# A two-layer transformer: the gated network's last product moved from VectorE to POOL, with a PSUM copy on ScalarE

## The chip, the core and the metric

One core of a Trainium2 chip runs the kernel: TensorE (PE, with its weight loads shown as PEld), VectorE (DVE), ScalarE (ACT), GpSimd (POOL) and SyncE (SP), which here only issues DMAs. The metric is the device time of one execution in microseconds, the median of several runs. POOL reads and writes SBUF only in this kernel; PE writes the eight PSUM banks of 128x512 f32, and DVE and ACT read them.

## What is computed

The input is 8 sequences of 256 tokens with 128 features. Two layers follow each other, and each is attention and then a feed-forward network, both with a residual sum. The last network is the gated one that the change touches:

```python
# layer 0: x = x + attention0(layernorm(x));  x = x + relu(layernorm(x) @ W1 + b1) @ W2 + b2
# layer 1: x = x + attention1(layernorm(x)), 16 heads of 8, not causal
def _L1_ffn_ref(x, w_gate, w_up, w_down):      # HIDDEN = 384
    wg = _dequant(w_gate, x.dtype)             # integers times 1/127
    wu = _dequant(w_up, x.dtype)
    wd = _dequant(w_down, x.dtype)
    gate = jnp.einsum('bsd,hd->bsh', x, wg)
    up = jnp.einsum('bsd,hd->bsh', x, wu)
    h = jax.nn.silu(gate) * up
    return jnp.einsum('bsh,dh->bsd', h, wd)
# x = x + _L1_ffn_ref(layernorm(x), ...)
```

## The kernel before

The kernel is written engine by engine; each engine's program is a fixed order of instructions, and semaphores hold the engines to each other. Nothing is scheduled by a planner.

The work runs in phases `i = -1 .. 18`. Phases 0 to 7 carry the attention of layer 0 for sequences 0 to 7, phases 8 to 15 that of layer 1. Each phase has 16 slots `s`, one for each head. In a slot, PE writes the scores of the next phase's head s (`scores`, lines 812 to 816, three banks in turn) and the transposed, shifted scores of this phase's head s (`shifted`, lines 834 to 838, two banks in turn). DVE takes the maxima of the first (`maximum`, L654 in layer 1), ACT the exponential of the second (`exp`, L497, output `PB`). Since there are two banks for the shifted scores, `shifted(i, s)` waits until the exponential of slot s-2 is done; since there are three for the scores, `scores(i+1, s)` waits for the maximum of slot s-3. After slots 6, 10 and 14, and in slot 1 of the next phase, PE multiplies four heads' probabilities by V (`pv`, L860).

The rest of a sequence's work is laid between the slots of the phases that follow its attention. For layer 1 it is this:

- one phase later (its attention being phase i-1): slot 3, PE turns the outputs (`turn_o`, L869) and DVE divides them (`norm_o`, L661 and L663, output `Y`); slot 4, POOL adds `Y` to the stream `xs` (L415); slot 5, DVE's statistics; slot 6, POOL's normalisation (`norm`, L351 to L361); slot 10, PE transposes (L765), ACT and DVE make the two f16 parts `XHL`;
- two phases later: in slots 3, 6 and 12 PE computes part j = 0, 1, 2 of the gated network (`ffn1_in`, L927: the gate half in columns 0 to 255 of a bank, the up half in columns 256 to 511) and ACT takes the tanh of the gate half (L554, output `TH`); in slots 4, 7 and 13 DVE does the part's two operations (`hidden`): `GA = (TH + 1) * gate` (L675) and `HG = GA * up` (L678), the second of which empties the bank;
- three phases later: slot 0, PE's last product (`ffn1_out`, L935), and DVE adds it to the stream (`add_stream`, L670). The store of the sequence waits for that sum.

So sequence c has its gated parts in phase c+10 and its last product in phase c+11. Phases 10 to 14 have all the work of a slot, phase 15 has no scores of a next phase any more, and phases 16, 17 and 18 have no attention at all: only the rest of sequences 5, 6 and 7. Parts 0, 1 and 2 use banks 7, 6 and 7; the turned outputs (`oT1`) and the transposed norm (`xT3`) use bank 6 too.

`GA` has two buffers, taken by `j % 2`. The silu is made of a tanh, since silu(g) = g (1 + tanh(g/2)) / 2; the constants are in the weights of the last product.

Of the kernel before, what the change touches and what calls it, by code (L numbers as in the profile page):

```python
# [7 lines left out]
ALU = mybir.AluOpType  # L8
# [8 lines left out]
P = 128  # L17
B, S, D = 8, 256, 128
# [73 lines left out]
def program(nc, x, w0, tab, small, w1, wint, ident, masks, out):  # L92
    with ExitStack() as ctx:
        def sb(name, shape, dt=F32):
            return ctx.enter_context(nc.sbuf_tensor(name, shape, dt))

        def sem(name):
            return ctx.enter_context(nc.semaphore(name))
# [55 lines left out]
        HR = sb("HR", [P, NI, S])  # L154
        TH = [sb(f"TH{j}", [P, S]) for j in range(NG)]
        GA = [sb(f"GA{j}", [P, S]) for j in range(2)]
        HG = sb("HG", [P, NG, S])


# [40 lines left out]
        s_res = sem("x_plus_attention_1")  # L200
        s_hr = sem("ffn0_hidden")
        s_xhi = sem("normedT_3_hi")
        s_th, s_ga = sem("gate_tanh"), sem("gate_silu")

        block = ctx.enter_context(nc.Block())

# [131 lines left out]
        def _(pool):  # L338
# [17 lines left out]
            def norm(n, b):  # L356
                p = b % 2
                rstd(n, b)
                pool.wait_ge(s_rstd[n], 3 * b + 3)
                for t in range(TPB):  # L360
                    ins = pool.tensor_scalar(XN[n][p][:, t], xs[:, b * TPB + t], NMN[:, n, p, t:t + 1],  # L361
                                             RS[:, n, p, t:t + 1], ALU.add, ALU.mult)
                ins.then_inc(s_xn[n], 1)
# [8 lines left out]
            def spread_v(i):  # L372
# [7 lines left out]
                                           va_(b).rearrange("q t (c f d) -> q t c f d", f=2, d=HD)[:, :, :, e])  # L380
                ins.then_inc(s_vp, 1)

            def cut(i, s):

                pool.wait_ge(s_e, H * i + s + 1)

                pool.tensor_tensor(HELD[:, s:s + 1], EPSC[:, 0, 0:1], EPSC[:, 0, 0:1], ALU.add)  # L387
                r = s % RING
                pr = PB[:, r - 1:r + 1].rearrange("q u (n k) -> q (u n) k", n=2)[:, :, 0:P]
                pool.affine_select(out=pr, in_=pr, compare_op=ALU.is_ge, fill=0.0, base=0, pattern=[[0, 4], [1, P]],  # L390
                                   channel_multiplier=-1).then_inc(s_cut, 1)
# [15 lines left out]
            for i in range(-1, NPH + 3):  # L407
                L0, L1, L2 = [phase(i - n)[0] for n in range(3)]
                b1, b2 = [phase(i - n)[1] for n in (1, 2)]
                for s in range(H):  # L410
# [7 lines left out]
                        pool.tensor_tensor(halves(ZG), halves(Y), row(gate_row), ALU.mult).then_inc(s_zg, 1)  # L418
                    if s == 6 and L1 == 1:
                        norm(3, b1)  # L420
                    if s == 7 and i + 1 < NPH:
                        spread_v(i + 1)
                    if s == 8 and L2 == 0:
# [20 lines left out]
        def _(act):  # L444
# [62 lines left out]
            for i in range(-1, NPH + 3):  # L507
                L1, L2 = [phase(i - n)[0] for n in (1, 2)]
                b1, b2 = [phase(i - n)[1] for n in (1, 2)]
                for s in range(H):  # L510
# [40 lines left out]
                    if s in (3, 6, 12) and L2 == 1:  # L551
                        j = (3, 6, 12).index(s)
                        act.wait_ge(*filled(f"gu{j}", b2))
                        act.activation(TH[j][:, :], psum(f"gu{j}", b2)[:, 0:S], ACT.Tanh, scale=0.5 * SCALE).then_inc(s_th, 1)  # L554
                    for b, a in STAGE_A.items():
                        if a["xT"] == H * i + s:
# [19 lines left out]
        def _(dve):  # L576
# [95 lines left out]
            def hidden(c, j):  # L672
                m = psum(f"gu{j}", c)
                dve.wait_ge(s_th, NG * c + j + 1)
                dve.scalar_tensor_tensor(out=GA[j % 2][:, :], in0=TH[j][:, :], scalar=1.0, in1=m[:, 0:S],  # L675
                                         op0=ALU.add, op1=ALU.mult).then_inc(s_ga, 1)
                dve.wait_ge(s_ga, NG * c + j + 1)
                dve.tensor_tensor(HG[:, j], GA[j % 2][:, :], m[:, S:2 * S], ALU.mult).then_inc(*empties(f"gu{j}", c))  # L678

            for i in range(-1, NPH + 3):  # L680
                L1, L2, L3 = [phase(i - n)[0] for n in (1, 2, 3)]
# [64 lines left out]
        def _(pe):  # L746
# [181 lines left out]
                ins.then_inc(*fills(f"gu{j}", c))  # L928

            def ffn1_out(c):  # L930
                pe.wait_ge(*emptied("gu2", c))
                m = into("dn", c)
                for t in range(TPB):
                    for n in range(NG):
                        ins = pe.matmul(m[:, t * D:(t + 1) * D], HG[:, n, t * P:(t + 1) * P], WD[:, n],  # L935
                                        start=(n == 0), stop=(n == NG - 1))
                ins.then_inc(*fills("dn", c))
# [112 lines left out]
```

## Time and profile before

| | us |
|---|---|
| median of 3 runs | 359.61 (358.93 to 360.91) |
| the profiled execution | 359.73 |
| its span in the trace | 358.0 |
| PE busy | 299.5 (84%) |
| DVE busy | 258.4 (72%) |
| ACT busy | 220.4 (62%) |
| POOL busy | 156.4 (44%) |

The span runs from the first instruction to the last; the 1.73 us between it and the execution's time lie around it. An engine's busy time is the union of its instructions. Matmuls are pipelined, and their ends are modelled: a row of a matmul that lasts 0.27 us may be followed by the next one 0.11 us later. So starts are read, not ends, where PE's pace is asked for. Rows of a timeline begin with the start and the duration in us; consecutive instructions of one line may be merged into one row (x2, x3), whose duration is that of the group. In brackets stands the engine's idle time before the row and what released it.

### The profile page before, as it was taken

What the parts mean: (1) busy time and instruction counts of PE and PEld (TensorE: products, weight loads), DVE (VectorE), ACT (ScalarE), POOL (GpSimd) and SP (SyncE); (2) the same over time, 40 slices, a digit from 0 to 9 for tenths busy, and PEclk for the clock granted to TensorE, in tenths of its full rate; (3) what the DMA queues carried; (4) which work ended last, traced back from release to release, by engine and by line L of the source; (5) the groups of instructions that cost most, each with busy time, mean ns of one, the idle gap of its engine ahead of it and who ended that gap; (6) DMA issues with size and microseconds to landing.
All of it is one profiled execution on the core that took longest, in us unless ns stands there. A gap on an engine that the chain in (4) does not pass through costs nothing.

```text
span 358.0 us, 8359 instructions
## 1 busy us (share of the span) xinstructions
PE 299.5 (84%) x2832; PEld 210.3 (59%) x2832; DVE 258.4 (72%) x1009; ACT 220.4 (62%) x493; POOL 156.4 (44%) x367
## 2 busy tenths in 40 slices
PE   1761698696988989898989899999999999998754
PEld 1541465464756657575757576666667675764443
DVE  5784679788586767676676758768988989883433
ACT  5354267767576665666665666767776767677501
POOL 6263447867485757657574715220230303022020
PEclk9996659999999999999999999999999999999966
DMA  7567222314111122323000010101111110100001
GB/s 207 211 160 182 69 62 82 106 46 125 35 42 58 38 74 68 98 64 97 7 2 30 2 54 3 53 25 52 38 42 31 37 39 25 39 1 17 16 0 29
DMA packets 23034, 21.19 MB, mean 59 GB/s; under 512 B 2896, under 2 KB 20048, under 8 KB 22992
## 3 DMA queue, kind: packets, MB, share of 16 engines
q1 hardware_dynamic: 22992, 20.66, 20.2%
q8 instruction: 23, 0.38, 0.5%
q14 instruction: 19, 0.16, 0.1%
HBM read 13.18 MB, written 7.34 MB: 57 GB/s over the span
## 4 chain that ended last, share of the span: by engine, by line
PE 57%; DVE 14%; POOL 11%; ACT 9%; issue 7%; DMA 1%; POOLq 0%; ACTq 0%; SPq 0%; DVEq 0%
PE bank L860 14%; PE bank L834 5%; PE bank L892 4%; PE bank L901 4%; PE bank L935 4%; PE bank L815 3%; PE bank L838 3%; PE bank L779 3%; ACT PB L497 3%; POOL PB L390 3%; PE bank L816 3%; PE bank L927 3%; DVE JUNK L651 3%; PE bank L909 2%; DVE STAT L588 2%
## 5 line engine op out<-in xcount | busy, mean ns | idle before, releaser
L497 ACT ACTIVATE PB<-bank 128x384 f32<-128x384 f32 (+1 forms) x256 | 131.2, 547 | 35.3 <-PE bank L836 18.3
L654 DVE TENSOR_REDUCE NM<-bank 128x2 f32<-128x512 f32 x128 | 82.2, 682 | 16.2 <-PE bank L816 16.0
L834 PE MATMUL bank<-QS,KS 128*128 128x256 f16 x256 | 70.2, 275 | 7.5 <-ACT PB L497 6.2
L860 PE MATMUL bank<-PB,VP 128*32 128x256 f32 (+1 forms) x1024 | 61.7, 358 | 9.1 <-POOL PB L390 9.1
L649 DVE CUSTOM_DVE_ANT_0 JUNK<-bank,MSF 128x128 bf16<-128x128 f32 x128 | 36.3, 283 | 26.7 <-PE bank L813 26.4
L651 DVE CUSTOM_DVE_ANT_0 JUNK<-bank,MSF 128x256 bf16<-128x256 f32 x128 | 53.7, 419 | 0.0
L860 PEld LDWEIGHTS bank<-PB,VP 128*32 128x32 f32 x1024 | 26.7, 109 | 32.5 <-POOL PB L390 12.4
L390 POOL TENSOR_SCALAR_AFFINE_SELECT PB<-PB 128x512 f32<-128x512 f32 x64 | 41.6, 650 | 0.0
L415 POOL TENSOR_TENSOR xs<-xs,Y 128x256 f32<-128x256 f32 x8 | 5.8, 728 | 77.7 <-DVE Y L663 77.7
L834 PEld LDWEIGHTS bank<-QS,KS 128*128 128x128 f16 x256 | 24.5, 96 | 21.9 <-ACT PB L497 19.6
L815 PE MATMUL bank<-KS,QS 96*128 96x256 f16 x128 | 35.2, 275 | 0.8 <-DVE NM L654 0.8
L813 PE MATMUL bank<-KS,QS 96*128 96x256 f16 x128 | 35.2, 281 | 0.0
L765 PE MATMUL bank<-IDF,XN 128*128 128x128 f32 x64 | 14.2, 306 | 24.7 <-POOL XN L361 12.0
L816 PE MATMUL bank<-KS,QS 96*128 96x256 f16 x128 | 34.6, 271 | 0.0
L838 PE MATMUL bank<-QS,KS 128*128 128x256 f16 x128 | 34.4, 271 | 0.0
L812 PE MATMUL bank<-KS,QS 96*128 96x128 f16 x128 | 29.0, 228 | 3.5 <-DVE NM L651 3.3
L387 POOL TENSOR_TENSOR HELD<-EPSC 128x1 f32<-128x1 f32 x64 | 15.3, 238 | 37.8 <-ACT PB L497 37.6
L836 PE MATMUL bank<-QS,KS 128*128 128x128 f16 x128 | 27.8, 217 | 0.0
L670 DVE TENSOR_TENSOR xs<-xs,bank 128x256 f32<-128x256 f32 x24 | 10.1, 420 | 24.3 <-PE bank L901 12.6
L361 POOL TENSOR_SCALAR XN<-xs,NMN,RS 128x128 f32<-128x128 f32 x56 | 24.7, 451 | 2.9
L351 POOL TENSOR_TENSOR VE<-MV,EPSC 128x2 f32<-128x2 f32 x32 | 6.3, 196 | 43.2 <-DVE MV L592 43.0
L765 PEld LDWEIGHTS bank<-IDF,XN 128*128 128x128 f32 x64 | 7.4, 149 | 29.1 <-POOL XN L361 15.2
(89 smaller groups left out, 619.4 us busy)
## 6 DMA issues: line engine op xcount, KB each, us to landing
scr<-PR SPq DMA_DIRECT2D x16, 256.0 KB, 2.8
QS<-scr SPq DMA_DIRECT2D x16, 128.0 KB, 2.6
QS<-scr SPq DMA_DIRECT2D x32, 64.0 KB, 2.9
KS<-scr SPq DMA_DIRECT2D x32, 64.0 KB, 2.9
KS<-scr SPq DMA_DIRECT2D x16, 128.0 KB, 3.0
scr<-PR SPq DMA_DIRECT2D x16, 128.0 KB, 1.9
out_x<-xs SPq DMA_DIRECT2D x8, 128.0 KB, 1.9
W<-in_w SPq DMA_DIRECT2D x1, 576.0 KB, 6.4
```

Source lines behind the costliest of these rows:

```text
L390: pool.affine_select(out=pr, in_=pr, compare_op=ALU.is_ge, fill=0.0, base=0, pattern=[[0, 4], [1, P]], channel_multiplier=-1).then_inc(s_c ...
L497: act.activation(PB[:, s % RING, 0:n], TB_[s % 2][:, 0:n], ACT.Exp).then_inc(s_e, 1)
L649: dve.tensor_tensor_reduce(JUNK[:, g % 3, 0], o[:, 0:P], MSF[:, 1], -1.0, 3e38, ALU.add, ALU.min, accum_out=m[:, s, 0:1])
L651: dve.tensor_tensor_reduce(JUNK[:, g % 3, 1:3], o[:, P:3 * P].rearrange("q (n k) -> q n k", n=2), MSF[:, :], -1.0, 3e38, ALU.add, ALU.min, ...
L654: dve.tensor_reduce(m[:, s, 0:2], o[:, :].rearrange("q (n k) -> q n k", n=2), AX.X, ALU.max, negate=True).then_inc(s_mx, 1)
L812: pe.matmul(o[:, 0:P], q[:, 0:P], k[:, 0:P], start=True, stop=True)
L813: ins = pe.matmul(o[:, P:3 * P], q[:, P:2 * P], k[:, :], start=True, stop=True)
L815: pe.matmul(o[:, 0:S], q[:, 0:P], k[:, :], start=True, stop=True)
L816: ins = pe.matmul(o[:, S:2 * S], q[:, P:2 * P], k[:, :], start=True, stop=True)
L834: pe.matmul(o[:, 0:S], k[:, 0:P], q[:, :], start=True, stop=True)
L838: ins = pe.matmul(o[:, S:2 * S], k[:, P:2 * P], q[:, :], start=True, stop=True)
L860: ins = pe.matmul(o, v, pr, start=(g % 2 == 0 and kt == 0), stop=True, skip_group_check=True)
```

## The change

For each of the three parts, ACT first copies the up half of the bank into a new SBUF tile `UP` and then takes the tanh as before. DVE keeps only `GA = (TH + 1) * gate`, and this operation now empties the bank. The product `HG = GA * UP` is POOL's, in slots 4, 8 and 13 (`gate_up`). `UP` and `GA` have two buffers each, taken by the running number of the part, n = 3c + j. ACT's copy and DVE's operation of part n wait for POOL's product of part n-2 (`s_hg`), POOL's product waits for the bank to be emptied and, as the one tile `HG` is written again, for the last product of the sequence before. The last product on PE waits for POOL's third product of the sequence.

```diff
+        UP = [sb(f"UP{j}", [P, S]) for j in range(2)]
...
+            def gate_up(c, j):
+
+                n = NG * c + j
+                pool.wait_ge(*emptied(f"gu{j}", c))
+                if n >= NG:
+                    pool.wait_ge(*filled("dn", c - 1))
+                pool.tensor_tensor(HG[:, j], GA[n % 2][:, :], UP[n % 2][:, :], ALU.mult).then_inc(s_hg, 1)
...
+                    if s in (4, 8, 13) and L2 == 1:
+                        gate_up(b2, (4, 8, 13).index(s))
...
                         act.wait_ge(*filled(f"gu{j}", b2))
+                        if NG * b2 + j >= 2:
+                            act.wait_ge(s_hg, NG * b2 + j - 1)
+                        act.copy(UP[(NG * b2 + j) % 2][:, :], psum(f"gu{j}", b2)[:, S:2 * S])
                         act.activation(TH[j][:, :], psum(f"gu{j}", b2)[:, 0:S], ACT.Tanh, scale=0.5 * SCALE).then_inc(s_th, 1)
...
                 dve.wait_ge(s_th, NG * c + j + 1)
-                dve.scalar_tensor_tensor(out=GA[j % 2][:, :], in0=TH[j][:, :], scalar=1.0, in1=m[:, 0:S],
-                                         op0=ALU.add, op1=ALU.mult).then_inc(s_ga, 1)
-                dve.wait_ge(s_ga, NG * c + j + 1)
-                dve.tensor_tensor(HG[:, j], GA[j % 2][:, :], m[:, S:2 * S], ALU.mult).then_inc(*empties(f"gu{j}", c))
+                if NG * c + j >= 2:
+                    dve.wait_ge(s_hg, NG * c + j - 1)
+                dve.scalar_tensor_tensor(out=GA[(NG * c + j) % 2][:, :], in0=TH[j][:, :], scalar=1.0, in1=m[:, 0:S],
+                                         op0=ALU.add, op1=ALU.mult).then_inc(*empties(f"gu{j}", c))
...
             def ffn1_out(c):
-                pe.wait_ge(*emptied("gu2", c))
+                pe.wait_ge(s_hg, NG * c + NG)
```

How the engines' programs stand, at the places of which the prediction speaks. First ACT in slots 3 to 7 of a phase with gated parts, before (`bank3` and `bank4` hold the shifted scores, `bank7` and `bank6` the gated parts 0 and 1):

```order
365 L497 ACTIVATE PB<-bank4 128x512 [waits pv_groups,shifted_scores]
366 L554 ACTIVATE TH0<-bank7 128x256 [waits bank7_filled]
367 L497 ACTIVATE PB<-bank3 128x512 [waits pv_groups,shifted_scores]
368 L497 ACTIVATE PB<-bank4 128x512 [waits pv_groups,shifted_scores]
369 L497 ACTIVATE PB<-bank3 128x512 [waits pv_groups,shifted_scores]
370 L554 ACTIVATE TH1<-bank6 128x256 [waits bank6_filled]
371 L497 ACTIVATE PB<-bank4 128x512 [waits pv_groups,shifted_scores]
```

And the same slots of the changed kernel (`hidden_1` is the semaphore of POOL's products):

```order
368 L508 ACTIVATE PB<-bank4 128x512 [waits pv_groups,shifted_scores]
369 L567 COPY UP1<-bank7 128x256 [waits hidden_1,bank7_filled]
370 L568 ACTIVATE TH0<-bank7 128x256
371 L508 ACTIVATE PB<-bank3 128x512 [waits pv_groups,shifted_scores]
372 L508 ACTIVATE PB<-bank4 128x512 [waits pv_groups,shifted_scores]
373 L508 ACTIVATE PB<-bank3 128x512 [waits pv_groups,shifted_scores]
374 L567 COPY UP0<-bank6 128x256 [waits hidden_1,bank6_filled]
375 L568 ACTIVATE TH1<-bank6 128x256
376 L508 ACTIVATE PB<-bank4 128x512 [waits pv_groups,shifted_scores]
```

The copy stands between the exponential of the slot and the tanh, so the exponential of the next slot comes two operations after it in place of one.

POOL at its program's end, before: the last sequence's sum, its normalisation, and nothing behind it.

```order
361 L415 TENSOR_TENSOR xs<-xs,Y 128x256 [waits bank6_emptied]
362 L351 TENSOR_TENSOR VE<-MV,EPSC 128x2 [waits variance_3]
363 L352 TENSOR_TENSOR NMN<-MV,EPSC 128x2
364 L354 TENSOR_TENSOR RS<-VE,EPSC 128x2 [waits rstd_3]
365 L361 TENSOR_SCALAR XN31<-xs,NMN,RS 128x128 [waits rstd_3]
366 L361 TENSOR_SCALAR XN31<-xs,NMN,RS 128x128
```

And of the changed kernel:

```order
379 L424 TENSOR_TENSOR xs<-xs,Y 128x256 [waits bank6_emptied]
380 L390 TENSOR_TENSOR HG<-GA0,UP0 128x256 [waits bank6_filled,bank7_emptied]
381 L352 TENSOR_TENSOR VE<-MV,EPSC 128x2 [waits variance_3]
382 L353 TENSOR_TENSOR NMN<-MV,EPSC 128x2
383 L355 TENSOR_TENSOR RS<-VE,EPSC 128x2 [waits rstd_3]
384 L362 TENSOR_SCALAR XN31<-xs,NMN,RS 128x128 [waits rstd_3]
385 L362 TENSOR_SCALAR XN31<-xs,NMN,RS 128x128
386 L390 TENSOR_TENSOR HG<-GA1,UP1 128x256 [waits bank6_filled,bank6_emptied]
387 L390 TENSOR_TENSOR HG<-GA0,UP0 128x256 [waits bank6_filled,bank7_emptied]
388 L390 TENSOR_TENSOR HG<-GA1,UP1 128x256 [waits bank6_filled,bank7_emptied]
389 L390 TENSOR_TENSOR HG<-GA0,UP0 128x256 [waits bank6_filled,bank6_emptied]
390 L390 TENSOR_TENSOR HG<-GA1,UP1 128x256 [waits bank6_filled,bank7_emptied]
```

One product came in between the sum and the normalisation of sequence 7, and five behind it: two of sequence 6 and the three of sequence 7.

## Rows read from the trace of the kernel before

**Rows 1.** The page: busy time, share of the span and count of each engine.
```profile
PE 299.5 (84%) x2832; PEld 210.3 (59%) x2832; DVE 258.4 (72%) x1009; ACT 220.4 (62%) x493; POOL 156.4 (44%) x367
```

**Rows 2.** Windows: stretch, length, busy PE PEld DVE ACT POOL, PE clock, DMA, GB/s.
```profile
280.00:300.00 20.00, 19.97 (x212) 12.96 (x214) 18.16 (x46) 14.54 (x31) 5.29 (x15) 1.00 0.13 36
```

**Rows 3.** Waits from 190 to 340 us: who for whom, total, times, longest.
```profile
PEld bank L834 <- ACT PB L497: 10.6, 32, 0.8
...
PEld bank L815 <- DVE NM L654: 3.1, 10, 0.7
```

**Rows 4.** Timeline of PE, phase 13 (slots 6, 9, and the next 0).
```profile
295.22 0.27 PE L816 MATMUL bank<-KS,QS 96*128 96x256 f16 x1
295.52 0.28 PE L834 MATMUL bank<-QS,KS 128*128 128x256 f16 x1
...
298.59 0.28 PE L834 MATMUL bank<-QS,KS 128*128 128x256 f16 x1
...
305.12 1.05 PE L935 MATMUL bank<-WD,HG 128*128 128x128 f32 x8
```

**Rows 5.** Timeline of ACT, phase 13, slots 3 to 6 and 12 to 14.
```profile
294.43 0.38 ACT L554 ACTIVATE TH<-bank 128x256 f32<-128x256 f32 x1 [0.23 <-PE bank L927]
294.87 1.68 ACT L497 ACTIVATE PB<-bank 128x512 f32<-128x512 f32 x3
...
302.72 0.40 ACT L554 ACTIVATE TH<-bank 128x256 f32<-128x256 f32 x1
302.98 1.12 ACT L497 ACTIVATE PB<-bank 128x512 f32<-128x512 f32 x2
```

**Rows 6.** Timeline of DVE, phase 13, slot 13.
```profile
303.40 0.41 DVE L675 SCALAR_TENSOR_TENSOR GA<-TH,bank 128x256 f32<-128x256 f32 x1
```

**Rows 7.** Timeline of ACT, phase 15, slots 3 to 6 and 12.
```profile
325.01 0.38 ACT L554 ACTIVATE TH<-bank 128x256 f32<-128x256 f32 x1
325.29 1.67 ACT L497 ACTIVATE PB<-bank 128x512 f32<-128x512 f32 x3
...
332.63 0.41 ACT L554 ACTIVATE TH<-bank 128x256 f32<-128x256 f32 x1
```

**Rows 8.** Timeline of PE, phase 15, slot 6, and phase 16, slot 0.
```profile
325.94 0.28 PE L834 MATMUL bank<-QS,KS 128*128 128x256 f16 x1 [0.46 <-ACT PB L497]
...
334.37 1.50 PE L935 MATMUL bank<-WD,HG 128*128 128x128 f32 x12
```

**Rows 9.** Timeline of DVE, phase 16, slot 3.
```profile
338.45 0.42 DVE L663 TENSOR_TENSOR Y<-bank,REC 128x256 f32<-128x256 f32 x1
```

**Rows 10.** Timeline of POOL, phase 16, slots 4 and 6.
```profile
338.96 0.73 POOL L415 TENSOR_TENSOR xs<-xs,Y 128x256 f32<-128x256 f32 x1 [9.75 <-DVE Y L663]
340.58 0.20 POOL L351 TENSOR_TENSOR VE<-MV,EPSC 128x2 f32<-128x2 f32 x1 [0.89 <-DVE MV L592]
```

**Rows 11.** Instructions that use HG: the product's own row (min/median/max ns).
```profile
L678 DVE TENSOR_TENSOR HG<-GA,bank x24: 420/421/422, 248.7 to 352.2; 128x256 f32<-128x256 f32 x24
```

**Rows 12.** Timeline of PE from phase 17 to the end.
```profile
345.56 2.93 PE L935 MATMUL bank<-WD,HG 128*128 128x128 f32 x12 [1.38 <-DVE HG L678]
...
350.73 0.61 PE L927 MATMUL bank<-XHL,WGU 128*128 128x256 f16 x4 [0.69 <-DVE HG L678]
352.72 2.57 PE L935 MATMUL bank<-WD,HG 128*128 128x128 f32 x12 [1.38 <-DVE HG L678]
```

**Rows 13.** Timeline of DVE in phases 16 and 17.
```profile
344.63 0.42 DVE L675 SCALAR_TENSOR_TENSOR GA<-TH,bank 128x256 f32<-128x256 f32 x1 [0.44 <-ACT TH L554]
...
350.25 0.42 DVE L678 TENSOR_TENSOR HG<-GA,bank 128x256 f32<-128x256 f32 x1
```

**Rows 14.** Timeline of ACT in phase 17: the first tanh of sequence 7.
```profile
349.38 0.38 ACT L554 ACTIVATE TH<-bank 128x256 f32<-128x256 f32 x1 [4.79 <-PE bank L927]
```

**Rows 15.** Windows, columns as in Rows 2: a microsecond of each of the two products.
```profile
346.00:347.00 1.00, 1.00 (x6) 1.00 (x6) 0.00 (x0) 0.00 (x0) 0.00 (x0) 0.50 0.00 0
...
353.00:354.00 1.00, 1.00 (x7) 1.00 (x7) 0.00 (x0) 0.00 (x0) 0.00 (x0) 0.57 0.00 0
```

More of the change, by code:

```diff
@@ L202, in program @@
         s_xhi = sem("normedT_3_hi")
-        s_th, s_ga = sem("gate_tanh"), sem("gate_silu")
+        s_th, s_hg = sem("gate_tanh"), sem("hidden_1")
         block = ctx.enter_context(nc.Block())
```

## The prediction

> **What bounds the kernel now.** I read the page first, then the windows of the stretch in which the gated network runs, then the waits, and last the timelines of single phases. The page gives DVE 258.4 us of a span of 358.0 and ACT 220.4 [rows 1], and these shares do not say which of them PE waits for. The window of 280 to 300 us lies in the full phases: DVE is busy for 18.16 us of 20, ACT for 14.54, POOL for 5.29, and the clock of PE is at 1.00 [rows 2]. By that view VectorE looks nearly full and POOL nearly empty, which is what the change would use.
>
> The waits say otherwise. From 190 to 340 us, PE's weight loads stood for 10.6 us in 32 waits for ACT's exponentials, and for 3.1 us in 10 waits for DVE's maxima [rows 3]. The reader should see in the timeline where: in phase 13 the scores' second matmul of slot 6 starts at 295.22, and the shifted scores, which at the pace of 0.11 us could start at 295.33, start at 295.52 [rows 4]. They need the exponential of slot 4, which is the first of the three that start at 294.87 with a common duration of 1.68 us [rows 5], so each takes about 0.60 and the first ends near 295.47. In slot 9 the shifted scores start at 298.59 [rows 4] behind the exponential of slot 7 in the same way. So at the two places of a phase where a gated part stands just ahead of an exponential, ACT is what PE waits for, though ACT has the more idle time of the two. Between these places PE runs without a gap, and a delay that it gets there is not caught up.
>
> **The change, part by part.** The sum is made against the profiled execution, 359.73 us (span 358.0), 0.12 above the median of the runs; I treat the two as one.
>
> What DVE loses: 24 products of 0.42 us [rows 11], 10.1 us, three in each of eight sequences. I cost this gain at nothing in the full phases. What would be late next, if DVE were never late, is the exponential: in both places above PE stands at a shifted-scores matmul, whose releaser is ACT. The bound on the other side is the 3.1 us of waits for the maxima [rows 3].
>
> What ACT gains: 24 copies of 128x256 from PSUM. The row nearest to it is the tanh of the same shape from the same bank, 0.38 us, whose successor starts 0.28 us [rows 7] or 0.26 us [rows 5] after it. So a copy ahead of the tanh delays what follows by 0.26 to 0.28; I take 0.27. The upper bound is 0.38, no overlap at all; less than nothing is excluded, as the copy is an additional instruction in ACT's order. By the Trainium skill (ScalarE: Activation LUTs, section Table sets: the hidden batching unit) an activation with immediate operands takes 186 ns and 0.833 ns an element, and back-to-back ones overlap by 93 ns: for 256 columns an estimate of 0.40 us, and 0.31 for the following start. The trace's 0.26 to 0.28 is a little less; by the page the sum below would be about 0.8 us higher.
>
> Full phases (10 to 14): the tanh starts at 294.43 and the exponential at 294.87 [rows 5], 0.44 later and not 0.27, since its scores are ready only then. Copy and tanh together take 0.54, so the exponential starts 0.54 - 0.44 = 0.10 late, and PE's slot 6 with it; I take 0.09, since with the pitch of 0.26 it is 0.08 and with 0.28 it is 0.12. The part at slot 6 repeats the pattern (again 0.44 between tanh and exponential). The third, at slot 12, costs nothing: the exponential behind it starts at 302.98 [rows 5], is needed by the shifted scores of slot 15 only, and between these lies a whole probabilities-times-V group; its cover is over half a microsecond. Five phases by two by 0.09: **+0.9 us** (0.8 to 1.2; at 0.38 for the copy, 0.38 + 0.27 - 0.44 = 0.21 each, 2.1).
>
> Phase 15: PE writes no further scores, the tanh starts at 325.01 and the exponential at 325.29 directly behind it [rows 7], and PE stands for 0.46 us until 325.94 for that exponential [rows 8]. Here there is no slack, so both places cost the full 0.27: **+0.54 us**.
>
> POOL in the full phases: its products cost 0.73 us each, by the sum of the same shape [rows 10], and begin 0.09 us behind DVE (338.45 + 0.42 = 338.87, then 338.96) [rows 9, 10]. The last of a phase: DVE's operation starts at 303.40 [rows 6]; the tanh ahead of it, now at 302.72 + 0.27 [rows 5], ends at 303.39, so 303.43 at the earliest; + 0.41 + 0.09 + 0.73 = 304.66, and PE wants it at 305.12 [rows 4]. Slack 0.46, cost 0. POOL is busy 5.29 of 20 us [rows 2], so its three products, 2.2 us a phase, delay nothing there.
>
> The last product of sequence 5 has less room. The tanh of its sequence's last part starts at 332.63 [rows 7]: + 0.27 + 0.41 + 0.04 (tanh to DVE) = 333.35, + 0.42 + 0.09 + 0.73 + 0.05 (to PE) = 334.64. PE began at 334.37 [rows 8]. The shift that both have from the earlier terms cancels, so **+0.27 us**, and behind it in PE's order stands the last probabilities-times-V group, on which all the rest hangs.
>
> Phase 16: POOL's new product of sequence 6, part 0, is queued between the last sum and the last normalisation. Copy and tanh let DVE begin it about 0.3 us later, at 339.2; it ends at 339.6. POOL's sum ends at 338.96 + 0.73 = 339.69, the product then at about 340.45, and the normalisation starts at 340.58, when DVE's statistics are there [rows 10]. It fits with 0.1 us to spare: cost 0, up to 0.2.
>
> The end, first piece: DVE's operation on part 2 of sequence 6 starts at 344.63 [rows 13] and PE's last product at 345.56 [rows 12], 0.93 later. Now 0.42 + 0.09 + 0.73 + 0.05 = 1.29 from the one to the other, and the copy is ahead of the tanh: 0.36 + 0.27 = **+0.63 us**.
>
> The end, second piece, sequence 7. The first tanh stood at 349.38 [rows 14]. Copy 0.27, tanh 0.38 and 0.04 for the step: DVE at 350.07, bank 7 is free at 350.48, where before the product of 350.25 freed it at 350.67 [rows 13] and PE went on at 350.73 [rows 12]. PE is thus 0.2 us early with part 2, done near 351.14, but POOL's first product, from 350.57 to 351.30, holds the copy of part 2, which has to wait for its `UP` buffer: 351.34. Copy 0.27, tanh 0.38, step 0.04, DVE 0.41, step 0.09, POOL 0.73, step 0.05: 353.31 in place of 352.72 [rows 12], **+0.59 us**. POOL's 0.73 us [rows 10] against DVE's 0.42 [rows 11] is 1.7 times. The Trainium skill (GPSIMD Engine Reference, section 4.1, Engine selection) speaks against the change here: it names VectorE for elementwise products and puts two-input operations on GpSimd at about twice the time. By twice, 0.84, four products stand in these serial pieces, and the sum would be 0.44 higher.
>
> The clock of PE at the end: in 346 to 347 us, within the product of phase 17, the granted clock is 0.50 of full, 1.2 GHz; in 353 to 354 it is 0.57 [rows 15], so it fell from 2.4 GHz just after the last product had begun. That product took 2.57 us, the one of phase 17 took 2.93 for the same twelve matmuls [rows 12]. PE now idles 0.8 us longer ahead of it, so I take it at the lower clock from its start: **+0.36 us** (0 to 0.36).
>
> Sum: 0.9 + 0.54 + 0.27 + 0.63 + 0.59 + 0.36 = 3.29 us; 359.73 + 3.29 = **363.0 us**. The bounds of the forecast: 2.8 without the clock's term and with the lower ends, 3.8 with the upper.
>
> **Rivals.** *The copy is not overlapped* (0.38 for what follows). Full phases 2.1, phase 15 0.76, sequence 5 0.38, first piece 0.74, second piece 0.59 + 0.22 = 0.81, clock 0.36: 5.15, so 364.9. For it: a copy with a wait on two semaphores has no row here. Against it: every operation of that shape on ACT lets the next start after 0.26 to 0.28.
>
> *ACT's delays are absorbed in the phases.* If the maxima come early enough that PE works ahead of the slots, only the serial rest remains: 0.27 + 0.63 + 0.59 + 0.36 = 1.85, so 361.6, or 361.2 with the clock as before. For it: DVE gets 1.3 us free in each phase. Against it: the shifted scores of slot s cannot be ahead of the exponential of slot s-2.
>
> *VectorE is the real bound* (the kernel gets faster). At 18.16 of 20 us [rows 2] DVE runs behind from slot 4 to slot 10, and if the slots behind slot 7 are late by its backlog and not by the exponentials, the 3.1 us of its waits go [rows 3], ACT's delays being covered by them: -3.1 + 1.85 = -1.25, so 358.5, and 358.1 with the clock as before. It decides if PE's places in slots 8 to 10 move forward against slot 6. Against it: the shifted scores of slot 9 start with the end of slot 7's exponential.
>
> **How the numbers follow.** The forecast has 0.62, the copy without overlap 0.18, the absorbed delays 0.15, VectorE as the bound 0.05. Half a per cent, 1.8 us, is about what a measurement of this kernel can tell from no change: slower means over 361.4, faster under 357.8. The absorbed case falls on both sides of 361.4, and 0.05 of the forecast may fall under it: same 0.14, faster 0.02, slower 0.84. The range reaches from 361.0, within the absorbed case, to 364.9.
>
> **What would show it.** In the changed trace: the exponential behind the first tanh of a full phase 0.5 us or more behind the copy's start; each of the full phases, from one last product to the next, 0.18 us longer than in the trace of before; PE's wait for ACT in phase 15 longer by 0.27 at two places; DVE's busy time down by 10 us, ACT's up by some 7 to 9, POOL's by 17.5; between the start of DVE's last operation and the last product 1.3 us. I am wrong if the phases keep their length or shrink, if the copy hides within PE's time, or if POOL's product takes well over 0.73 us.

## The result, and the profile of the changed kernel

| | before | changed |
|---|---|---|
| median of 7 runs, us | 359.61 (358.93 to 360.91) | 363.12 (361.82 to 363.40) |
| ratio | | 1.0081, 95% interval 1.0063 to 1.0099 |
| profiled execution, us | 359.73 | 361.82 |
| its span, us | 358.0 | 359.8 |

The changed kernel is slower by 0.8 per cent, clear of the interval: by the ratio 2.9 us (2.3 to 3.6), by the medians 3.5. The forecast was 363.0 us.

The work went where the change sends it. The page of the changed kernel, busy time of each engine, against [rows 1]:

```profile
PE 298.8 (83%) x2832; PEld 210.7 (59%) x2832; DVE 250.1 (70%) x985; ACT 225.9 (63%) x517; POOL 173.7 (48%) x391
```

DVE has 24 instructions and 8.3 us less, ACT 24 and 5.5 us more, POOL 24 and 17.3 us more. The window of 280 to 300 us, against [rows 2] (columns as there: busy PE, PEld, DVE, ACT, POOL, then PE's clock), shows the same in the full phases, at the same full clock:

```profile
280.00:300.00 20.00, 19.58 (x208) 13.10 (x210) 16.92 (x41) 14.99 (x35) 8.58 (x20) 1.00 0.13 34
```

DVE is now busy for 16.92 us of 20 in place of 18.16, and the phases are longer all the same. The waits from 190 to 340 us, against [rows 3], say for whom (L848 are the shifted scores, L508 the exponentials, L829 the scores, L668 the maxima):

```profile
PEld bank L848 <- ACT PB L508: 12.8, 34, 1.1
...
PEld bank L829 <- DVE NM L668: 2.3, 5, 0.7
```

The waits for the maxima fell from 3.1 to 2.3 us, and those for the exponentials rose from 10.6 to 12.8.

Phase 13 in the timeline of ACT, against [rows 5]: L567 is the new copy, L568 the tanh.

```profile
294.50 0.37 ACT L567 COPY UP<-bank 128x256 f32<-128x256 f32 x1 [0.23 <-PE bank L941]
294.77 0.39 ACT L568 ACTIVATE TH<-bank 128x256 f32<-128x256 f32 x1
295.05 1.68 ACT L508 ACTIVATE PB<-bank 128x512 f32<-128x512 f32 x3
```

And of PE, against [rows 4]:

```profile
295.29 0.27 PE L830 MATMUL bank<-KS,QS 96*128 96x256 f16 x1
295.70 0.28 PE L848 MATMUL bank<-QS,KS 128*128 128x256 f16 x1
...
298.88 0.28 PE L848 MATMUL bank<-QS,KS 128*128 128x256 f16 x1
...
305.40 1.50 PE L949 MATMUL bank<-WD,HG 128*128 128x128 f32 x12
```

The copy starts where the tanh started, the tanh 0.27 later, the exponential 0.28 after that: 0.55 in place of 0.44. PE's step from the scores to the shifted scores in slot 6 is 0.41 in place of 0.30. The part at slot 6 adds the same again, and the phase ends 0.22 later.

### The profile page after: what moved, and what is told of

Its sections match the earlier page's. It is cut to its first block, busy times and chain, and to the rows that moved or that the text cites. A ratio compares the mean times of both kernels' runs of the same rounds, so it can differ in the third digit from the quotient of the medians.

```text
span 359.8 us, 8448 instructions
## 1 busy us (share of the span) xinstructions
PE 298.8 (83%) x2832; PEld 210.7 (59%) x2832; DVE 250.1 (70%) x985; ACT 225.9 (63%) x517; POOL 173.7 (48%) x391
## 4 chain that ended last, share of the span: by engine, by line
PE 52%; DVE 13%; POOL 12%; ACT 11%; issue 9%; DMA 1%; POOLq 0%; ACTq 0%; SPq 0%; DVEq 0%
PE bank L874 13%; ACT PB L508 5%; PE bank L848 4%; PE bank L906 4%; PE bank L915 4%; PE bank L949 4%; POOL PB L399 3%; PE bank L793 3%; DVE JUNK L665 3%; PE bank L852 2%; PE bank L829 2%; PE bank L941 2%; PE bank L923 2%; PE bank L830 2%; DVE STAT L602 2%
## 5 line engine op out<-in xcount | busy, mean ns | idle before, releaser
L508 ACT ACTIVATE PB<-bank 128x384 f32<-128x384 f32 (+1 forms) x256 | 131.4, 549 | 33.1 <-PE bank L850 18.4
L668 DVE TENSOR_REDUCE NM<-bank 128x2 f32<-128x512 f32 x128 | 83.6, 683 | 22.0 <-PE bank L830 21.2
L848 PE MATMUL bank<-QS,KS 128*128 128x256 f16 x256 | 70.2, 275 | 9.3 <-ACT PB L508 6.9
L848 PEld LDWEIGHTS bank<-QS,KS 128*128 128x128 f16 x256 | 24.5, 96 | 23.8 <-ACT PB L508 21.9
L829 PE MATMUL bank<-KS,QS 96*128 96x256 f16 x128 | 35.1, 274 | 0.8 <-DVE NM L668 0.8
L390 POOL TENSOR_TENSOR HG<-GA,UP 128x256 f32<-128x256 f32 x24 | 17.5, 731 | 30.8 <-DVE GA L691 30.7
L793 PE MATMUL bank<-XT,W 128*128 128x256 f32 x64 | 22.4, 504 | 4.0 <-ACT XT L469 3.9
```

The lines of the kernel that those rows point to most:

```text
L508: act.activation(PB[:, s % RING, 0:n], TB_[s % 2][:, 0:n], ACT.Exp).then_inc(s_e, 1)
L668: dve.tensor_reduce(m[:, s, 0:2], o[:, :].rearrange("q (n k) -> q n k", n=2), AX.X, ALU.max, negate=True).then_inc(s_mx, 1)
L793: ins = pe.matmul(m[:, half * S:(half + 1) * S], w, XT[0][b % 2][:, :], start=True, stop=True)
L829: pe.matmul(o[:, 0:S], q[:, 0:P], k[:, :], start=True, stop=True)
L848: pe.matmul(o[:, 0:S], k[:, 0:P], q[:, :], start=True, stop=True)
```

## The stages of all the kernels

A whole time of 360 us is a poor measure for 0.2 us a phase, but the starts of the last products are not. They divide the profile into stages; this table is made from the timelines of PE (first matmul of one product to the first of the next; "begin" is the start of the first turned outputs, "rest" is from the start of sequence 7's product to the span's end).

| kernel | begin | full phases 11 to 13 | phase 14 | phase 15 | seq. 5 to 6 | seq. 6 to 7 | rest |
|---|---|---|---|---|---|---|---|
| before | 72.87 | 15.73 | 15.51 | 13.74 | 11.19 | 7.16 | 5.28 |
| before, again (e5) | 73.33 | 15.73 | 15.51 | 13.75 | 10.62 | 7.32 | 4.37 |
| changed | 72.26 | 15.95 | 15.74 | 14.56 | 11.35 | 7.79 | 4.96 |
| changed, again (e4) | 73.40 | 15.96 | 15.73 | 14.56 | 11.99 | 8.03 | 4.29 |
| e1, copy alone | 72.34 | 15.96 | 15.73 | 14.30 | 11.83 | 8.13 | 5.69 |
| e2, no product | 72.38 | 15.73 | 15.51 | 13.74 | 10.83 | 6.25 | 4.30 |
| e3, copy on DVE | 73.33 | 15.73 | 15.62 | 14.16 | 11.39 | 7.72 | 5.17 |
| e6, DVE for seq. 5 to 7 | 72.13 | 15.96 | 15.73 | 13.75 | 11.28 | 6.80 | 5.60 |
| e7, copies in slack | 73.53 | 15.73 | 15.51 | 14.01 | 11.42 | 7.80 | 5.60 |
| e8, e6 and e7 together | 72.82 | 15.73 | 15.51 | 13.75 | 11.04 | 7.16 | 5.09 |

The middle columns repeat to 0.01 us from one execution to another, and between kernels that have the same work there; they belong to the program. The first and the three last do not: within one and the same program "begin" moves by up to 1.1 us and a stage of the end by up to 0.9, where the granted clock of PE changes. For "begin" the windows of 20 to 40 us show it: the four executions with a begin over 73.3 have a mean granted clock of 0.67 or 0.68 there, the six others 0.71 to 0.74. The changed kernel, its first execution and its second:

```profile
20.00:40.00 20.00, 10.21 (x48) 7.41 (x47) 13.50 (x40) 10.29 (x21) 7.73 (x16) 0.72 0.68 159
...
20.00:40.00 20.00, 10.26 (x38) 7.85 (x39) 12.52 (x34) 9.84 (x21) 8.00 (x17) 0.68 0.69 163
```

Whether the lower clock is the cause of the later begin, or both come of something else, no run settles. With two executions of each, these columns account for the 0.9 us between the spans of the two of before and the 1.3 us between the two of the changed kernel.

## The experiments

Theory A: the full phases pay for the place of the copy, ahead of the tanh and so ahead of exponentials on which PE waits; the end pays for a serial chain that became longer. Theory B: POOL's products cost the full phases. Theory C: DVE was what bounded the full phases.

### e4 and e5: the changed kernel and the one before, again

No edit. For e4:

> The changed kernel once more, unchanged, to see how far its time and the lengths of its stages repeat. If the stage lengths belong to the program, the full phase is 15.95 and phase 15 is 14.56 again whatever the whole time; the beginning (up to 60 us) and the last product, where the granted clock of PE moves, may differ by up to 1.3 us, so 361.8 to 363.4.

Measured: 362.30 us (361.55 to 363.41), ratio 1.0077 (1.0056 to 1.0098); full phase 15.96, phase 15 14.56. For e5:

> The kernel before once more, to see which of its stages repeat. If theory A's reading of stages is fair: full phases 15.73 to 15.74 and phase 15 13.74 again; the beginning and the matmuls of the end at whichever clock PE is granted there; 359.0 to 360.9 us in all.

Measured: 359.61 us, ratio 1.0007 (0.9991 to 1.0022), stages as expected. From these four profiles come the pairs of executions, below, in which the clock of one stage is the same.

### e1: the copy alone

```diff
                         act.wait_ge(*filled(f"gu{j}", b2))
+                        act.copy(UP[(NG * b2 + j) % 2][:, :], psum(f"gu{j}", b2)[:, S:2 * S])
                         act.activation(TH[j][:, :], psum(f"gu{j}", b2)[:, 0:S], ACT.Tanh, scale=0.5 * SCALE).then_inc(s_th, 1)
```

> The kernel before with ACT's copy of the up half ahead of each tanh and nothing else: DVE still does both operations, nothing reads the copy. Theory A (ACT's place in the order is what the full phases pay for): a full phase 15.95 us in place of 15.74 (first matmul of one last product to the next, sequence 3 to 4), phase 15 (sequence 4's to 5's) 14.3 in place of 13.74, and from sequence 5's to 7's last product 0.27 + 0.27 longer; in all +2.1 to +2.4 us, some 362. Theory B (POOL's product, by waiting or by its traffic in SBUF, costs the full phases): full phases stay at 15.74, in all +1.1 at most. Theory C (DVE's load matters): full phases longer than in the changed kernel, over 15.95, as DVE keeps its product here.

Measured: 362.82 us, ratio 1.0083 (1.0061 to 1.0105). Full phase 15.96 and phase 15 14.30, as theory A has them, with DVE doing all that it did before and POOL nothing new. In the timeline of ACT, phase 13:

```profile
294.52 0.37 ACT L555 COPY UP<-bank 128x256 f32<-128x256 f32 x1 [0.23 <-PE bank L929]
294.78 0.39 ACT L556 ACTIVATE TH<-bank 128x256 f32<-128x256 f32 x1
295.06 1.69 ACT L498 ACTIVATE PB<-bank 128x512 f32<-128x512 f32 x3
```

These are the rows of the changed kernel to 0.02 us. So the 0.22 of a full phase is the copy's, whole: B and C fall for the full phases. Against the execution of before in the table the end was longer than expected, 1.6 us from sequence 5 to 7 in place of 0.54, and the whole was 3.0 us (2.2 to 3.8) longer in place of 2.1 to 2.4. About 0.26 of it is a term that I had not seen: DVE's product of sequence 6's part 0 stands ahead of sequence 7's statistics. From the start of `Y` to the statistics it is 1.54 us here:

```profile
339.54 0.42 DVE L665 TENSOR_TENSOR Y<-bank,REC 128x256 f32<-128x256 f32 x1
340.28 0.42 DVE L677 SCALAR_TENSOR_TENSOR GA<-TH,bank 128x256 f32<-128x256 f32 x1 [0.31 <-ACT TH L556]
340.74 0.42 DVE L680 TENSOR_TENSOR HG<-GA,bank 128x256 f32<-128x256 f32 x1
341.08 0.29 DVE L590 BATCH_NORM_STATS2 STAT<-xs 128x6 f32<-128x128 f32 x1
```

In the changed kernel it is 1.27 (339.88 to 341.15), since the product is POOL's. 0.4 of the remaining 0.8 us is seen in one place: gated part 2 of sequence 7 took 1.03 us in this execution, at the lower clock, and 0.61 in that of before. The rest one profile does not settle.

### e2: DVE without its product

```diff
-                dve.scalar_tensor_tensor(out=GA[j % 2][:, :], in0=TH[j][:, :], scalar=1.0, in1=m[:, 0:S],
-                                         op0=ALU.add, op1=ALU.mult).then_inc(s_ga, 1)
-                dve.wait_ge(s_ga, NG * c + j + 1)
-                dve.tensor_tensor(HG[:, j], GA[j % 2][:, :], m[:, S:2 * S], ALU.mult).then_inc(*empties(f"gu{j}", c))
+                dve.scalar_tensor_tensor(out=HG[:, j], in0=TH[j][:, :], scalar=1.0, in1=m[:, 0:S],
+                                         op0=ALU.add, op1=ALU.mult).then_inc(*empties(f"gu{j}", c))
```

> The kernel before without the multiplication by the up half: DVE writes (TH+1)*gate straight to HG, so it is free of 24 operations of 0.42 us and of the wait between the two; ACT and POOL as before. What it leaves out is that product. Theory A: full phases unchanged at 15.74 within 0.05 and phase 15 at 13.74, a gain of 0.45 for each of the two serial pieces at the end and nothing else: -0.9 us, some 358.9. Theory C (DVE was the bound of the full phases): each of the five full phases shorter by 0.3 or more, in all -2.5 us or more, 357 or less.

Measured: 357.00 us, ratio 0.9930 (0.9916 to 0.9944). Read by the whole time alone, -2.5 us, this would have confirmed theory C. The stages refute it: full phase 15.73, phase 15 13.74, not 0.01 shorter than before. PE in phase 13, slots 6 and 9 (L814 and L832 are scores and shifted scores):

```profile
294.68 0.27 PE L814 MATMUL bank<-KS,QS 96*128 96x256 f16 x1
294.98 0.28 PE L832 MATMUL bank<-QS,KS 128*128 128x256 f16 x1
...
297.74 0.27 PE L814 MATMUL bank<-KS,QS 96*128 96x256 f16 x1
298.04 0.28 PE L832 MATMUL bank<-QS,KS 128*128 128x256 f16 x1
```

The step in slot 6 is 0.30 as in [rows 4]: DVE is free of its product, and PE stands at the same place for ACT. Against the profile of before in the table, most of the gain (2.25 us of 2.8) is in the last three columns. The serial part of it is seen in what PE waits between its matmuls at the end, 0.93 us ahead of each last product where [rows 12] have 1.38: 0.45 each, as expected. The rest, some 1.6 us by the median, stays open. The last product took 1.60 us in this execution and not 2.57, which is clock; but e5, whose last product took 1.60 as well, has 22.31 us in its last three columns to e2's 21.38, and that difference of 0.93 is the serial part alone. The other 0.95 us between e2 and e5 lies in "begin", which the edit does not touch.

### e3: the copy on DVE

```diff
-                        if NG * b2 + j >= 2:
-                            act.wait_ge(s_hg, NG * b2 + j - 1)
-                        act.copy(UP[(NG * b2 + j) % 2][:, :], psum(f"gu{j}", b2)[:, S:2 * S])
...
                     dve.wait_ge(s_hg, NG * c + j - 1)
+                dve.tensor_copy(UP[(NG * c + j) % 2][:, :], m[:, S:2 * S])
```

> The changed kernel with the copy of the up half done by DVE behind the tanh, so ACT's program is the one of before and POOL keeps the products. Theory A: full phases back to 15.74, phase 15 to 13.74, sequence 5's last product 0.33 late, and at the end the serial pieces cost 0.70 and 0.59 (copy and operation on DVE, then POOL's 0.73): about +1.6 us, some 361.3. Theory B (POOL's product costs the full phases): they stay at 15.95 and the whole stays at +3 us.

Measured: 362.23 us, ratio 1.0074 (1.0059 to 1.0089). Full phases 15.73: with POOL's 24 products in place and ACT's program as before, they cost nothing. Theory B falls here too. But the products of sequences 4 and 5 waited for POOL, phase 14 by 0.11 and phase 15 by 0.42 us. The whole is 1 us worse than I expected: the ratio says 2.7 us (2.1 to 3.2) in place of 1.6. From phase 14 to sequence 7's last product the stages add up to 1.3 us more than in one execution of before and to 1.7 more than in the other. That difference stays open. As a way to build the kernel it is no better than the changed one.

### e6: POOL for sequences 0 to 4 only

```diff
+LATE = 5
...
+                        if b2 < LATE:
                             act.copy(UP[(NG * b2 + j) % 2][:, :], psum(f"gu{j}", b2)[:, S:2 * S])
...
+                if c < LATE:
+                    ins.then_inc(*empties(f"gu{j}", c))
+                    return
+                ins.then_inc(s_ga, 1)
+                dve.wait_ge(s_ga, n + 1 - NG * LATE)
+                dve.tensor_tensor(HG[:, j], GA[n % 2][:, :], m[:, S:2 * S], ALU.mult).then_inc(*empties(f"gu{j}", c))
```

> The changed kernel for sequences 0 to 4 and the way of before (no copy, both operations on DVE) for sequences 5, 6 and 7, whose gated parts lie in phases 15, 16 and 17. Theory A: full phases 15.95, phase 15 back at 13.74, the end as before: 5 times 0.22 = +1.1 us, some 360.7. A rival, that the loss lies in the serial end and in phase 15 alone and the full phases only look longer: within 0.4 us of before.

Measured: 361.01 us, ratio 1.0051 (1.0031 to 1.0072). Phase 15 back at 13.75, full phases still 15.96: by the stages, five times 0.22, 1.1 us of the loss lies in the full phases, and the rival falls. The ratio gives 1.8 us (1.1 to 2.6); expected were 1.1, and what lies above is not assigned.

### e7: the copies where ACT has slack

```diff
+def moved(c, j):
+
+    return c < 6 and j < 2
...
+                    if s in (6, 8) and L2 == 1 and moved(b2, s // 8):
+                        j = s // 8
+                        act.wait_ge(s_ga, 2 * b2 + j + 1)
+                        if NG * b2 + j >= 2:
+                            act.wait_ge(s_hg, NG * b2 + j - 1)
+                        act.copy(UP[(NG * b2 + j) % 2][:, :],
+                                 psum(f"gu{j}", b2)[:, S:2 * S]).then_inc(*empties(f"gu{j}", b2))
```

The lines left out move POOL's products of these parts to slots 7 and 9 and let DVE's operation hand the bank on to the copy.

> The changed kernel with the same 24 copies on ACT, but for sequences 0 to 5 the copies of parts 0 and 1 stand behind the exponentials of slots 6 and 8, on which PE doesn't wait, in place of ahead of the tanh; the bank is then emptied by the copy, and POOL's product of part 0 stands behind its normalisation. Theory A (what is paid is the copy's place ahead of the exponentials of slots 4 and 7): full phases back to 15.74 within 0.03, phase 15 at 14.0 (only sequence 5's last product waits, 0.27), the end as in the changed kernel: 1.05 + 0.54 = 1.6 us less than the changed kernel, some 361.3. A rival (ACT's total work, or POOL's, in a phase is what counts): full phases stay at 15.9 or more.

Measured: 361.26 us, ratio 1.0055 (1.0034 to 1.0076); full phases 15.73, phase 15 14.01. By the stages the repair is worth 1.65 us, five times 0.22 and 0.55, as expected; the ratios of whole times, 1.0055 against 1.0081 and 1.0077, give 0.8 to 0.9, with intervals too wide (each 0.6 us or more to either side) to tell this from 1.65. The same operations on the same engine cost 0.22 us a phase in one place and nothing in the other. In phase 13, L538 is the copy, L585 the tanh:

```profile
295.08 0.38 ACT L585 ACTIVATE TH<-bank 128x256 f32<-128x256 f32 x1 [0.23 <-PE bank L958]
295.52 1.68 ACT L517 ACTIVATE PB<-bank 128x512 f32<-128x512 f32 x3
297.09 0.37 ACT L538 COPY UP<-bank 128x256 f32<-128x256 f32 x1
298.14 0.38 ACT L585 ACTIVATE TH<-bank 128x256 f32<-128x256 f32 x1 [0.68 <-PE bank L958]
```

The exponentials are again 0.44 behind the tanh, and the copy stands in time in which ACT had nothing to do: the idle time ahead of the second tanh is 0.68 now, 0.27 less than before, where the row is

```profile
297.50 0.38 ACT L554 ACTIVATE TH<-bank 128x256 f32<-128x256 f32 x1 [0.95 <-PE bank L927]
```

This settles theory A for the full phases.

### e8: both repairs

The edits of e6 and e7 together, with `moved` for `c < LATE`.

> The two repairs together: for sequences 0 to 4 POOL has the products, with the copies of parts 0 and 1 behind the exponentials of slots 6 and 8; for sequences 5, 6 and 7 the way of before. So 15 of the 24 products are still POOL's and 15 of the copies still ACT's. Theory A says that nothing is then left to pay: full phases 15.73, phase 15 13.75, the whole within 0.5 us of before, 359.1 to 360.1. If something of the change costs that the stages did not show (POOL's traffic, the semaphores, another clock of PE), it stays 1 us or more above.

Measured: 359.45 us against 359.45, ratio 1.0004 (0.9989 to 1.0020). With 15 of the 24 products on POOL and 15 copies on ACT the kernel is as fast as before, within 0.7 us. So the two places account for the loss, nothing else of the change costs anything that is seen here, and the time taken off DVE in the full phases is worth nothing: they are 15.73 us again.

### e9 to e11: the end, reordered

The end, where over a third of the loss lay, is a serial chain, and a microsecond may be had there. e9 goes back to the kernel before and puts the three gated parts of sequence 7 on PE ahead of sequence 6's last product:

```diff
+            if (name, L, b) == ("dn", 1, 6):
+                s = 13
+            if (L, b) == (1, 7) and name in ("gu2", "dn"):
+                k = ("gu2", "dn").index(name)
...
-                    if s == 0 and L3 == 1:
+                    if s == (13 if b3 == 6 else 0) and L3 == 1:
                         ffn1_out(b3)
```

DVE's sum of sequence 6 moves behind sequence 7's parts in the same way, and sequence 7 gets an `HG` tile of its own.

> The kernel before with another order at its end: the three gated parts of sequence 7 stand on PE ahead of sequence 6's last product in place of behind it, with a second HG tile and with banks 0 and 1, free by then, for part 2 and the last product of sequence 7. If the serial chain at the end (product, tanh, two operations, product) is what the end costs, the tanh and DVE's operations of sequence 7 now run under sequence 6's last product: the last product starts 1.9 us earlier, 357.5 to 358.0 in all. If the lower clock of PE there rules, the gain is under 1 us.

Measured: 358.72 us, ratio 0.9982 (0.9964 to 1.0000), a third of what I expected. The timeline of PE at its end:

```profile
345.59 2.72 PE L934 MATMUL bank<-XHL,WGU 128*128 128x256 f16 x12 [1.47 <-DVE HG L685]
348.92 4.99 PE L942 MATMUL bank<-WD,HG 128*128 128x128 f32 x24 [0.62 <-DVE HG L685]
```

Sequence 6's product waited 0.62 us for bank 6, which held sequence 7's part 1. e10 puts it in bank 2:

```diff
             if (name, L, b) == ("dn", 1, 6):
-                s = 13
+                s, k = 13, 2
```

> The reordered end of before with sequence 6's last product in bank 2, which is free by then, in place of bank 6, for which it waited 0.62 us until DVE had emptied sequence 7's part 1. If that wait is the reason why the reordering brought 0.65 us and not 1.9, the product starts 0.6 us earlier and the whole is 0.6 lower, some 358.1; if the lower clock of PE there sets the end, nothing or little is gained, 358.7.

Measured: 356.47 us, ratio 0.9922 (0.9898 to 0.9946), 2.8 us under before. The execution that was profiled took 360.72 us, with a granted clock of 0.908 on the mean and of 0.95 even in the full phases, where the others have 1.00; so its stages are not compared. e11 is the same kernel:

> The kernel with the reordered end and the free bank once more, since its profiled execution had a mean granted clock of 0.908 where all others lie from 0.947 to 0.962. Expected: full phases 15.73 and phase 15 13.75 as in before, sequence 6's last product directly behind the 12 matmuls of sequence 7's gated parts, and the whole 2.5 to 3.2 us under before, 356.3 to 357.0.

Measured: 356.10 us against 359.02, ratio 0.9919 (0.9899 to 0.9939). Its end:

```profile
345.76 2.72 PE L935 MATMUL bank<-XHL,WGU 128*128 128x256 f16 x12 [1.47 <-DVE HG L686]
348.27 3.96 PE L943 MATMUL bank<-WD,HG 128*128 128x128 f32 x24
```

The wait is gone, and the products run on without a gap. The gain over before, 2.8 and 2.9 us, is larger than the 1.3 us expected of e10. In the two profiles the missing wait is worth 0.65 us (348.92 to 348.27), and another 1.03 goes with the clock: the 24 matmuls took 3.96 us here and 4.99 in e9, and PE was back at full clock from 351 us here, which is 2.4 GHz, while e9 still stood at half of it, 1.2 GHz. First e11, then e9:

```profile
351.00:352.00 1.00, 1.00 (x12) 1.00 (x10) 0.35 (x1) 0.00 (x0) 0.00 (x0) 1.00 0.00 0
...
351.00:352.00 1.00, 1.00 (x6) 1.00 (x6) 0.14 (x1) 0.00 (x0) 0.00 (x0) 0.50 0.00 0
```

That the clock came back sooner because the pause was gone is not shown; these are single executions. This version beats both kernels.

## Why the prediction was right, point by point

The whole was right in sign, size and mechanism, but for one step, the clock's term. That 363.0 lies so near to the median of 363.12 is in part luck: by the ratio the loss is 2.9 us, so 362.5, and in the sum of 3.29 a term of 0.36 that was not there made up for about as much that was missing from the others. The steps, in its order:

**What bounds the full phases.** Right. e1 and e2 are the two halves of the claim: the copy alone lengthens them by the full amount, and freeing DVE alone shortens them by nothing. The 18.16 busy microseconds of 20 in [rows 2] were real and still not the bound. That PE runs "without a gap" between the two places is not quite so: in phase 13 of before the scores of slot 9 come 0.04 us behind the pace, and the shifted scores of slot 14 0.08.

**Full phases, +0.9.** Measured 5 x 0.22 = 1.1 (phase 10 too: from the turned outputs of its predecessor, 226.84 to 257.92 before and 226.24 to 257.54 changed, +0.22). The term was mis-sized by the choice of the pitch: I took 0.09 a place, it was 0.11, copy to tanh 0.27 and tanh to exponential 0.28, so 0.55 - 0.44. The side sum by a pitch of 0.31, 0.8 us higher, does not come out either: 0.04 more at each of the sixteen places of the sum (ten, two, one, one and two) is 0.6 us, and about 1.0 if the tanh of the full phases takes 0.31 too.

**Phase 15, +0.54 and +0.27.** Measured 0.82 together. ACT has no slack there, as read from [rows 7], and the copy costs its full pitch each time. Against [rows 7] and [rows 8], first ACT, then PE:

```profile
325.52 0.37 ACT L567 COPY UP<-bank 128x256 f32<-128x256 f32 x1
325.79 0.39 ACT L568 ACTIVATE TH<-bank 128x256 f32<-128x256 f32 x1
326.07 1.68 ACT L508 ACTIVATE PB<-bank 128x512 f32<-128x512 f32 x3
```

```profile
326.73 0.28 PE L848 MATMUL bank<-QS,KS 128*128 128x256 f16 x1 [0.74 <-ACT PB L508]
...
335.70 1.60 PE L949 MATMUL bank<-WD,HG 128*128 128x128 f32 x12
```

PE's wait of 0.46 became 0.74. The last product began at 335.70, 0.26 after PE's turn of shifted scores was over (335.33 + 0.11); in e1, where DVE still makes the product, it began at 335.45, directly behind them. So the two terms are seen apart: phase 15 is 0.56 longer in e1, by the copies, and 0.26 more in the changed kernel, by POOL.

**POOL hidden in the full phases.** Right. In phase 13 its product of part 2 was over at 304.95, and PE wanted it at 305.40:

```profile
299.83 0.73 POOL L390 TENSOR_TENSOR HG<-GA,UP 128x256 f32<-128x256 f32 x1
304.22 0.73 POOL L390 TENSOR_TENSOR HG<-GA,UP 128x256 f32<-128x256 f32 x1 [3.65 <-DVE GA L691]
```

**Phase 16 at no cost.** Right: the product ended at 341.84, the normalisation began at 342.00, 1.62 us after the sum (340.38), as in [rows 10]. e1 shows in addition what the product on POOL saved here: with a copy and the product left on DVE, the statistics are 0.26 later.

**The end, first piece, +0.63.** From DVE's operation to PE's product it was 1.29 us, as forecast (0.93 before), and the copy 0.27 ahead of the tanh. The timeline of ACT:

```profile
345.07 0.37 ACT L567 COPY UP<-bank 128x256 f32<-128x256 f32 x1
345.34 0.39 ACT L568 ACTIVATE TH<-bank 128x256 f32<-128x256 f32 x1
```

of DVE and of POOL:

```profile
345.76 0.42 DVE L691 SCALAR_TENSOR_TENSOR GA<-TH,bank 128x256 f32<-128x256 f32 x1 [0.30 <-ACT TH L568]
```

```profile
346.27 0.73 POOL L390 TENSOR_TENSOR HG<-GA,UP 128x256 f32<-128x256 f32 x1 [1.47 <-DVE GA L691]
```

and of PE:

```profile
347.05 2.93 PE L949 MATMUL bank<-WD,HG 128*128 128x128 f32 x12 [2.01 <-POOL HG L390]
...
352.03 0.69 PE L941 MATMUL bank<-XHL,WGU 128*128 128x256 f16 x4 [0.35 <-DVE GA L691]
354.84 2.23 PE L949 MATMUL bank<-WD,HG 128*128 128x128 f32 x12 [2.12 <-POOL HG L390]
```

The stage from sequence 5 to 6 is only 0.16 longer than in the profile of before, but that compares two clocks: the gated part of sequence 6 there took 1.06 us before and 0.60 changed. Pairs of executions with the same length of that part give +0.73 (11.35 to 10.62, both 0.60) and +0.80 (11.99 to 11.19, both 1.06); some 0.1 of it is the product of sequence 5 itself, which took 1.60 us behind a wait and 1.50 without one.

**The end, second piece, +0.59.** Measured from the first operation on sequence 7's part 0 to the last product: 3.98 us (350.86 to 354.84) in place of 3.34, +0.64. In this execution the detail held too: PE went on with part 2 earlier, 0.35 us of waiting in place of 0.69, and then ACT's copy of part 2 waited for POOL's first product:

```profile
352.87 0.37 ACT L567 COPY UP<-bank 128x256 f32<-128x256 f32 x1 [0.50 <-POOL HG L390]
```

In the other two executions the piece was 4.21 us (e4) in place of 3.50 (e5), +0.71; there part 2 took 1.03 us at the lower clock, and the copy waited for PE and not for POOL.

**The clock's term, +0.36.** This step failed. I put the last product at the lower clock from its start; it took 2.23 us in one execution of the changed kernel and 1.60 in another, against 2.57 and 1.60 in two of before. So the term came out as -0.34 in one pair and as nothing in the other. The windows of the changed kernel show the clock falling within the product, later than in [rows 15]:

```profile
355.00:356.00 1.00, 1.00 (x8) 1.00 (x9) 0.00 (x0) 0.00 (x0) 0.00 (x0) 0.82 0.00 0
356.00:357.00 1.00, 1.00 (x6) 0.78 (x4) 0.00 (x0) 0.00 (x0) 0.00 (x0) 0.50 0.00 0
```

One execution does not give the clock of the end, and so no such term. Without it the sum was 2.93; with the measured terms it is 1.1 + 0.82 + 0.63 + 0.64 = 3.2, and 3.3 with the 0.1 of sequence 5's product, within the interval of 2.3 to 3.6.

**DVE's and ACT's busy time.** I expected DVE down by 10 us and ACT up by 7 to 9; it was 8.3 and 5.5. ACT's copies overlap with their neighbours, so 24 of them added less than 24 times 0.37. DVE's products did too: e2, which only takes them off, has 8.5 us less.

**The rivals.** The copy without overlap falls by the 0.27 to the tanh. The absorbed delays fall by the full phases, 15.95. VectorE as the bound falls by e2: with DVE free of its product the shifted scores of slot 9 start 3.06 us behind those of slot 6, and 3.07 in [rows 4].

## What to carry to other kernels

An engine that is busy nine tenths of the time need not be the bound, and one that is busy three quarters may be: look for the engine whose operation is last ahead of each of PE's gaps, and price an added operation by what stands behind it in its engine's order, not by its length. The same copy cost 0.11 us, 0.27 us or nothing depending on its slot. Where the pipeline runs out, an operation on the serial chain counts in full, and there the order of the work on PE, which is free to change, brought 2.9 us, while the balance between engines brought nothing.

## What the runs showed of the hardware

- PE's granted clock at the end is not a property of the program: the same twelve matmuls of the same kernel took 2.57 and 1.60 us in two executions. The beginning moved too (first turned outputs at 72.26 and at 73.40, mean granted clock 0.72 and 0.68 from 20 to 40 us). Such a difference is as large as the effects studied here; below 1 us only the lengths of stages at full clock were compared.
- A copy or tanh of 128x256 from PSUM on ACT lasts 0.37 to 0.43 us, mostly 0.37 to 0.39, and the next operation, if it waits for nothing, starts 0.25 to 0.28 us after its start, also behind a copy with two semaphores ahead of it. The Trainium skill (ScalarE: Activation LUTs, section What ACT_TABLE_LOAD costs, where the formula stands, and not the section that the prediction names) gives an estimate of 0.40 and 0.31 by its formula; here it was mostly less.
- POOL's product of 128x256 took 0.73 us beside DVE and ACT at work just as in the idle end (724 to 738 ns in all 24), 1.7 times DVE's 0.42, and it starts 0.09 us after DVE's end, where DVE starts some 0.03 after ACT's end and PE 0.05 after POOL's.
- Twelve f32 matmuls (128x128) at full clock took 1.60 us where they started behind a wait, and 1.50 directly behind other matmuls; at half the clock 2.93.
